# Cross-attention block with a mixture of experts: the dense expert stage is replaced by a two-phase dispatch of each token to its two experts

## The reference

```python
x = x + attention(layernorm(x), ctx, ctx, mask, Wq, Wk, Wv, Wo)
h = layernorm(x)
probs = softmax(h @ wg.T)                      # 8 experts
topk_w, topk_idx = top_k(probs, 2)
topk_w = topk_w / sum(topk_w)
expert_w = sum(one_hot(topk_idx, 8) * topk_w)  # zero for the six experts not chosen
y = sum over e of expert_w[e] * ((silu(h @ w1[e].T) * (h @ w3[e].T)) @ w2[e].T)
out = x + y
```

## Time and profile before

| | us |
|---|---|
| median of 3 runs (lowest, highest) | 327.93 (326.25, 330.78) |
| the profiled execution, own time | 327.75 |
| its span, first to last instruction | 325.9 |
| TensorE busy | 280.9 (86%) |
| VectorE busy | 262.5 (81%) |
| ScalarE busy | 176.2 (54%) |
| GpSimd busy | 125.1 (38%) |
| mean granted clock of TensorE, share of full speed | 0.966 |

### The profile page before, as it was taken

One profiled execution on the slowest core, in us unless ns is written; L12 is line 12 of the kernel. 1 busy time (PEld: TensorE's weight loads), 2 busy tenths in 40 slices (PEclk: granted clock), 3 DMA queues, 4 the chain that ended last, 5 costly groups with the idle time before them and its releaser, 6 DMA issues. The chain is left out here.

```text
span 325.9 us, 5240 instructions
## 1 busy us (share of the span) xinstructions
PE 280.9 (86%) x1689; PEld 209.9 (64%) x1689; DVE 262.5 (81%) x523; ACT 176.2 (54%) x312; POOL 125.1 (38%) x111
## 2 busy tenths in 40 slices
PE   1947788989898989798899889897898978999994
PEld 0823565667566757575668667785686856888882
DVE  6586965887588757797649999879998799999893
ACT  6891256546655665375664355552455534666551
POOL 5201250125011501131166556554565535666660
PEclk9995599999999999999997999999999999999998
DMA  5984503340333043430800003400134001240101
GB/s 151 283 232 100 126 2 82 91 120 3 93 87 81 2 96 84 111 119 18 257 4 1 0 1 108 155 0 0 34 112 149 0 2 32 88 173 2 32 0 32
DMA packets 32618, 24.96 MB, mean 77 GB/s; under 512 B 2984, under 2 KB 27184, under 8 KB 32592
## 3 DMA queue, kind: packets, MB, share of 16 engines
q1 hardware_dynamic: 31440, 23.08, 25.1%
q0 software_dynamic: 320, 1.05, 1.3%
q10 hardware_dynamic: 832, 0.51, 0.6%
HBM read 15.12 MB, written 1.11 MB: 50 GB/s over the span
## 5 line engine op out<-in xcount | busy, mean ns | idle before, releaser
L897 POOL TENSOR_TENSOR big<-big,raw 128x512 f32<-128x512 f32 x64 | 87.9, 1375 | 70.3 <-ACT big L819 59.0
L431 PE MATMUL bank<-st,bd 128*128 128x512 f32 x320 | 88.9, 402 | 11.8 <-DVE big L1205 11.7
L431 PEld LDWEIGHTS bank<-st,bd 128*128 128x128 f32 x320 | 58.3, 190 | 28.5 <-DVE big L1205 17.5
L660 ACT ACTIVATE st<-big 128x512 fp32r<-128x512 f32 x64 | 40.5, 632 | 50.3 <-DVE big L1205 49.7
L1180 DVE TENSOR_REDUCE m_neg<-bank 128x4 f32<-128x512 f32 x64 | 43.2, 682 | 20.3 <-PE bank L601 20.0
L1205 DVE TENSOR_TENSOR big<-big,bank 128x512 f32<-128x512 f32 x64 | 43.5, 679 | 12.0 <-POOL big L897 11.7
L632 PE MATMUL bank<-st,bd 128*128 128x512 f32 x150 | 51.8, 397 | 0.2 <-DVE m_bd L1193 0.2
L819 ACT ACTIVATE big<-bank 128x512 f32<-128x512 f32 x64 | 38.0, 593 | 24.7 <-PE bank L431 24.3
L1193 DVE TENSOR_TENSOR m_bd<-big,st 128x512 fp32r<-128x512 f32 x42 | 47.4, 1129 | 0.1
L790 ACT ACTIVATE big<-bank 128x512 f32<-128x512 f32 x64 | 37.5, 600 | 17.4 <-PE bank L587 17.1
L601 PE MATMUL bank<-bd,st 128*128 128x512 f32 x64 | 30.1, 496 | 7.0 <-DMA bd<-st 6.6
(11 more groups left out here) (119 smaller groups left out, 422.5 us busy)
## 6 DMA issues: line engine op xcount, KB each, us to landing
bd<-st SPq DMA_DIRECT2D x128, 64.0 KB, 2.1
raw<-ew_rows SPq DMA_DIRECT2D x32, 256.0 KB, 5.0
x_all<-in_x SPq DMA_DIRECT2D x4, 256.0 KB, 3.9
mask_i<-in_mask_BxS_if POOLq DMA_DIRECT2D x4, 256.0 KB, 4.5
ctx_all<-in_L_ffn_w SPq DMA_DIRECT2D x1, 1024.0 KB, 5.8
out<-ck SPq DMA_DIRECT2D x4, 256.0 KB, 2.3
ctx_all<-in_ctx SPq DMA_DIRECT2D x3, 256.0 KB, 4.4
ctx_all<-in_ctx ACTq DMA_DIRECT2D x1, 256.0 KB, 5.5
```

What stands on the lines that cost most here:

```text
L431: last = nc.tensor.matmul(o, w, m, start=(k == 0), stop=(k == len(pairs) - 1))
L660: return nc.scalar.activation(o, i, ACT.Copy)
L897: nc.gpsimd.tensor_tensor(silw[n % 3], sil[n % 3], ewb[:, k // 2, :], ALU.mult).then_inc(silw_ready, 1)
```

## The change

The attention rounds stay, and the expert stage is new. Each token is worked on only for its two experts. Its normalised row is scattered into a DRAM table at a place in its expert's region, together with the number of its (token, choice) pair in a 129th column; the table is then worked off in tiles of 128 rows, each of one expert; the results are scattered to DRAM by pair number, and at the end are gathered, weighted and added.

- There are two phases: the first takes quarters 0 to 2, the second quarter 3. As the number of tokens of an expert is not known when the program is built, each phase has as many tiles as could be needed in the worst case: (2\*1536 - 8)//128 + 8 = 31 and (2\*512 - 8)//128 + 8 = 15. All 46 are computed, whatever the counts. A tile past the end reads a block of filler rows.
- Routing on VectorE gets more steps: running sums of the selections over sequences (cum), which of the two choices each is (before, which), the row in the table (place_rows, with the counts of lower tokens from two products "rk" on TensorE), the weight of each choice (weigh), and per phase a table of the tiles, three parts (table). Routing of quarter 0 moves from the last round into the end of the round before it, that of quarters 1 and 2 from the expert stage into the last round, and that of quarter 3 lies beside the tiles 5 to 12. The normalised rows are written twice (two choices).
- In VectorE's last round the ticks now carry: place_rows(0) and the normalising of quarter 1 (tick 0), statistics of quarter 2 (1), weigh(0) (3), routing_step of quarter 1 (4 and 5), normalising of quarter 2 (7), place_rows(1) (8), weigh(1) (9), routing_step of quarter 2 (11 and 12), place_rows(2) and table part 0 (14), weigh(2) and part 1 (15), part 2 (16). Before they carried routing_step(0), the weights of quarter 0, and statistics and normalising of quarter 1 and statistics of quarter 2.
- GpSimd no longer multiplies. It issues 8 indirect DMAs a quarter (send) and one a tile (out to ys). The ones of quarter 3 are interleaved with tiles 5 to 12.
- SyncE opens a phase: 8 register values are loaded from `pad`, 9 DMAs of 128 rows of filler are issued, 31 (or 15) row numbers are loaded into registers, and the sends and the filler are waited for. Then it loads tiles, in a ring of XR = 8; tile n waits until the output of tile n - 8 has landed. The second phase is opened between tiles 23 and 24.
- TensorE, per tile: one transpose of the rows (turn_tile); for h1 and h3 together two products with 512 columns and two with 256 (hidden), where the tokens are now the stationary operand and the expert's matrix moves, its column from a register; two transposes of the gated result (turn_hidden); and six products with 128 columns of w2 moved, three for each half of the hidden channels (down), three tiles later.
- ScalarE, per tile: rounded copy of 128 columns, Silu of 256, rounded copy of 256, and a copy of the 128 columns that down has summed (take_rows).
- VectorE, per tile: two subtractions (128 and 256 columns) and the product of 256 columns.
- At the end SyncE gathers 8 pieces of 256 KB, VectorE does 32 operations of 128 columns, and four pieces are stored.

```diff
-LAG = 5
-RH = 6
+CT = 128
+PHASES = (3, NQ - 3)
+CAPS = [n * T for n in PHASES]
+NTS = [(2 * c - E) // CT + E for c in CAPS]
+NT = sum(NTS)
+XR, GR, YR = 8, 3, 6
...
 @block.sync
-            def spread_weights(q):
...
+            def open_phase(f):
+                sp.wait_ge(pad_ready, f + 1)
+                sp.dma_start(xg[f][E * REGS[f]:E * REGS[f] + CT, :], consts[:, C_PAD:C_PAD + RW]).then_inc(padded[f], 16)
+                _, at = nc.values_load_multi_w_load_instructions(pad[0:1, f, :], [mybir.EngineType.SP], ...)
+                for row in at:
+                    sp.dma_start(xg[f][bass.ds(row, CT), :], consts[:, C_PAD:C_PAD + RW]).then_inc(padded[f], 16)
+                sp.wait_ge(tab_ready, f + 1)
+                _, at = nc.values_load_multi_w_load_instructions(tab[0:1, 0, 32 * f:32 * f + NTS[f]], [mybir.EngineType.SP], ...)
+                for q in (range(3) if f == 0 else range(3, NQ)):
+                    sp.wait_ge(sent[q], 16 * 2 * QB)
+                sp.wait_ge(padded[f], 16 * (E + 1))
+                return list(at)
+            rows = open_phase(0)
+            for n in range(NT):
+                f = int(n >= NTS[0])
+                if n == NTS[0] - XR + 1:
+                    rows += open_phase(1)
+                if n >= XR:
+                    sp.wait_ge(t_full, n - XR + 1)
+                    sp.wait_ge(ysb_out[(n - XR) % YR], 16 * ((n - XR) // YR + 1))
+                sp.dma_start(xt[n % XR], xg[f][bass.ds(rows[n], CT), :]).then_inc(in_t[n % XR], 16)
...
 @block.tensor
+            def hidden(n):
+                pe.wait_ge(tlo_ready, n + 1)
+                if n >= 2:
                     pe.wait_ge(gg_ready, n - 1)
+                nc.tensor.matmul(both, t_lo[n % 2], first_high[:, :, bass.ds(col[n], I)], start=True, stop=False)
+                nc.tensor.matmul(both, t_hi[n % 2], first_high[:, :, bass.ds(col[n], I)], start=False, stop=False)
+                for k in range(2):
+                    last = nc.tensor.matmul(h[:, k * I:(k + 1) * I], t_hi[n % 2], first_low[k][:, bass.ds(col[n], I)],
+                                            start=False, stop=(k == 1))
+            def down(n):
+                pe.wait_ge(glo_ready, n + 1)
+                if n >= 1:
+                    pe.wait_ge(ysb_ready, n)
+                for c in range(2):
+                    piece = slice(c * P, (c + 1) * P)
+                    high, low = (second[:, k, bass.ds(col[n] + c * P, D)] for k in range(2))
+                    nc.tensor.matmul(yb[:, 0:D], g_hi[n % GR][:, piece], high, start=(c == 0), stop=False)
+                    nc.tensor.matmul(yb[:, 0:D], g_hi[n % GR][:, piece], low, start=False, stop=False)
+                    last = nc.tensor.matmul(yb[:, 0:D], g_lo[n % GR][:, piece], high, start=False, stop=(c == 1))
+            col = columns(0)
+            turn_tile(0)
+            for n in range(NT + 3):
+                if n + 1 < NT:
+                    turn_tile(n + 1)
+                if n == NTS[0]:
+                    col += columns(1)
+                if n < NT:
+                    hidden(n)
+                if n >= 3:
+                    down(n - 3)
+                if 1 <= n < NT + 1:
+                    turn_hidden(n - 1)
...
 @block.scalar
+            for n in range(NT + 3):
+                if n + 1 < NT:
+                    round_tile(n + 1)
...
+                    nc.scalar.activation(sil[n % 2], hb[n % 2][:, 0:I], ACT.Silu).then_inc(sil_ready, 1)
                 if n >= 3:
+                    take_rows(n - 3)
+                if 1 <= n < NT + 1:
                     round_hidden(n - 1)
...
 @block.gpsimd
+            for n in range(NT):
+                pool.wait_ge(ysb_ready, n + 1)
+                pool.wait_ge(in_t[n % XR], 16 * (n // XR + 1))
+                pool.indirect_dma_start(ys, bass.IndirectOffsetOnAxis(xt[n % XR][:, D:RW].bitcast(I32), 0), y_sb[n % YR], None, ...)
+                if 5 <= n < 5 + 2 * QB:
+                    send(QB * (NQ - 1) + (n - 5) // 2, (n - 5) % 2)
...
 @block.vector
+                            if tick == 0:
+                                place_rows(0)
+                                normalise(QB, NQ + 1)
...
+                            if tick == 14:
+                                place_rows(2)
+                                table(0, 0)
+                            if tick == 15:
+                                weigh(2)
+                                table(0, 1)
+                            if tick == 16:
+                                table(0, 2)
...
+            for b in range(B):
+                if b % QB == 0:
+                    dve.wait_ge(in_g[b // QB], 32)
+                own(nc.vector.scalar_tensor_tensor(acc[b % 2], got[:, 0, b, :], wgt[:, b, 0:1], x_all[:, b, :], ALU.mult, ALU.add))
+                ins = nc.vector.scalar_tensor_tensor(o_sb[:, b, :], got[:, 1, b, :], wgt[:, b, 1:2], acc[b % 2], ALU.mult, ALU.add)
```

More of the change, by code:

```diff
@@ L55 @@
 EPS = 1e-5
-LAG = 5
-RH = 6
 SH = 3
+CT = 128
[3 more added lines that the diff above has]
+NT = sum(NTS)
+NC = CAPS[0] // CT
+REGS = [c + CT for c in CAPS]
+RW = D + 1
+PAIRS = 2 * B * S
+IN_RANGE = "counts are at most the capacity of a region, and the table ends in a minimum with the last row or expert"
+XR, GR, YR = 8, 3, 6
 def split_constant(v):
@@ L183, in program @@
         wo_s = sb("wo_s", [P, D])
-        wg_hi = sb("wg_hi", [P, E], F32R)
-        wg_lo = sb("wg_lo", [P, E], F32R)
+        wgT = sb("wgT", [P, E])
+        cum = sb("cum", [P, B + 2, E])
+        before = sb("before", [P, QB, E])
+        which = sb("which", [P, QB, 2, E])
+        place = sb("place", [P, QB, E])
+        spread = sb("spread", [P, QB, 2, E])
+        rows_i = sb("rows_i", [P, B, 2], I32)
+        wgt = sb("wgt", [P, B, 2])
+        cnt = sb("cnt", [P, E])
+        tiles = sb("tiles", [P, E])
+        until = sb("until", [P, E])
+        tab = sb("tab", [P, 2, 48], I32)
+        pad = sb("pad", [P, 2, E], I32)
         bias_w = sb("bias_w", [P, P], F32R)
@@ new lines, in _ @@
+            rest_of_tile(0)
+            for n in range(NT + 1):
+                if n + 1 < NT:
+                    rest_of_tile(n + 1)
+                if n < NT:
+                    dve.wait_ge(sil_ready, n + 1)
+                    if n >= 2:
+                        dve.wait_ge(gT_full, n - 1)
+                    nc.vector.tensor_tensor(gg[n % 2], sil[n % 2], hb[n % 2][:, I:2 * I], ALU.mult).then_inc(gg_ready, 1)
+                if 1 <= n < NT + 1:
+                    rest_of_hidden(n - 1)
+                if n == 0:
+                    second_statistics(NQ - 1)
+                if n == 1:
+                    normalise(QB * (NQ - 1), 2 * NQ - 1)
+                if n == 5:
+                    routing_step(NQ - 1, 0)
+                    routing_step(NQ - 1, 1)
+                if n == 6:
+                    routing_step(NQ - 1, 2)
+                    routing_step(NQ - 1, 3)
+                if n == 8:
+                    place_rows(NQ - 1)
+                if n == 10:
+                    table(1, 0)
+                if n == 11:
+                    table(1, 1)
+                if n == 12:
+                    table(1, 2)
```

540 lines of the change are left out of this document (304 added, 236 removed).

## The result

The changed kernel takes 339.18 us (median of 4, 339.03 to 340.63) beside 328.31 for the kernel before (median of 4), a ratio of 1.034 with a 95% interval of 1.026 to 1.042. The forecast of 338 is met within its own range, but that the sum is met is luck: two of its terms are wrong by more than 10 us each and cancel. Measured again later, beside the last experiments, the changed kernel took 339.71 against 327.91, ratio 1.038 (1.035 to 1.041). One line of the profile's part 1 and four of its 40 slices of the changed kernel answer to the earlier trace rows. The profiled execution spans 339.0 us.

What follows compares the result with a forecast made beforehand. TensorE and VectorE were taken as bounds, counted stage by stage: first product at 187.7, tiles 114.1, extras 4, 6 and 3, end 21, sum 335.8, plus 1.85 outside the span: 338 us; own range 328 to 348, eight in ten 310 to 360.

Steps and rivals of the forecast that it cites:

- round 3, to `mT`: Attention round before the last: 7.3 us of VectorE work go in, about 2 us free, so +5 us.
- last round: Final attention round: VectorE's 37.5 us of work in a round of 27.2 us make it 13.3 us longer, bounds +7 to +20.
- With 3 us of its idle time left over: 40.5: Final attention round: VectorE has 37.5 us of work and keeps only 3 us idle, so the round takes 40.5 us.
- over 90% busy: Sign to look for in the final attention round: VectorE busy more than 90% of the time.
- the routing is hidden: Rival, attention rounds 3 and 4: VectorE's added work fits idle time, growth only 2 and 7 us, total 327; chance 0.15.
- I take that 0.22, as the row nearest in shape: Expert tiles on TensorE: each of six 128-column down products costs 0.22 us, 1.33 us a tile of 2.48.
- cheap products: Rival, expert tiles: down products cost 0.11 us, TensorE 1.82 a tile, ring decides at about 2.05, total 318; chance 0.25.
- The chain of 6.3 us: Tile loading: copy, GpSimd issue, write, SyncE issue and load take 6.3 us over 3.1 tiles, 2.03 a tile, just under TensorE.
- second opening: Before tile 24: SyncE issues nine fillers, waits and loads 23 registers; +6 us, with a TensorE hole of 5 us or more.
- The rival of 0.2 us a value: Rival, SyncE and TensorE at both phase openings: each register load takes 0.2 us, +6 us, total 344; chance 0.10.
- The end: After the last tiles: copy, output landing, gathers, 32 VectorE operations at 0.3 us and the last store take 21 us.
- the first tile at 188: Sign at the start of the expert stage: the first tile's product starts at about 188 us (187.7 in the sum).

Runs made afterwards that it cites:

- without the low product: The two products per tile of the rounded gated values with the low part of w2 left out of the changed kernel; 337.25 us, ratio 1.026.
- the kernel with both edits: Changed kernel with 15 ring places, second-phase fillers between loads of tiles 17 to 25, opening's waits at tile 31; 338.91 us on the second chip, 318.57 on the third.
- The run that was to separate the clock from the pieces: 49 unused 512-column products added to the changed kernel on TensorE, ahead of waits in the last round and before the first tile; 361.04 us, ratio 1.105.

## Why the prediction was right, and where it was wrong

The forecast's sum against the same places of the trace after:

| | forecast | measured | off by |
|---|---|---|---|
| round 3, to `mT` | +5 | +9.0 | +4 |
| last round | +13.3 | +24.8 | +11.5 |
| seam | +6 | +4.8 | -1 |
| first expert product | 187.7 | 201.94 | +14.2 |
| first to last `hidden`, 45 steps | 121.6 | 110.5 | -11.1 |
| last `hidden` to the end | 26.5 | 26.6 | 0 |
| span | 335.8 | 339.0 | +3.2 |

The forecast column of the tiles is 45 x 2.48 + 4 + 6; the last is 2.5 + 3 + 21. `mT` is what ends round 3; the timelines of VectorE before and after show it:

```profile
136.69 0.29 DVE L1093 COPY mT<-bank 128x128 f32<-128x128 f32 x1
```
```profile
145.64 0.29 DVE L1262 COPY mT<-bank 128x128 f32<-128x128 f32 x1
...
196.82 0.29 DVE L1121 TENSOR_TENSOR x_all<-bank,x_all 128x128 f32<-128x128 f32 x1 [1.64 <-PE bank L517]
```

**The last round: the step that failed first.** "With 3 us of its idle time left over: 40.5" held that VectorE would fill to the brim, "over 90% busy". Its work was counted nearly right; its idle time was not. Busy time by engine from `mT` to the end of attention, the kernel before and the changed kernel (columns as in the earlier trace rows):

```profile
136.69:163.40 26.71, 23.64 (x246) 17.23 (x245) 19.55 (x66) 17.50 (x38) 6.57 (x8) 1.00 0.44 131
```
```profile
145.64:197.11 51.47, 36.82 (x269) 28.16 (x267) 35.18 (x134) 21.02 (x43) 30.45 (x32) 0.73 0.19 49
```

VectorE is busy for 35.2 us, where the forecast had 37.5, but in a stretch of 51.5 us: 68%. Its idle time was 7.2 us and grew to 16.3, where the forecast let it shrink to 3. What the runs showed in its place: the routing lies in unbroken pieces, TensorE waits behind them for the division of a head, and VectorE then waits for TensorE's chain in turn. Timeline of TensorE, one of these waits in round 3 and two in the last round:

```profile
140.88 0.48 PE L512 MATMUL bank<-cst,on 128*128 128x128 f32 x1 [5.94 <-DVE on L1130]
...
183.09 0.47 PE L512 MATMUL bank<-cst,on 128*128 128x128 f32 x1 [3.26 <-DVE on L1130]
...
193.15 0.33 PE L512 MATMUL bank<-cst,on 128*128 128x128 f32 x1 [2.46 <-DVE on L1130]
```

Round 3 went over its +5 in the same way. VectorE's busy time from 108.5 us to `mT` rose by 7.0 us (21.1 to 28.1), close to the 7.3 that were counted, but its idle time grew from 7.1 to 9.0 us instead of giving 2 away. Routing of quarter 0 stands there from 133.18 to 140.18 us, and TensorE's wait of 5.94 us is behind it.

In the one execution that was profiled, 4.2 us of work more made the last round 4.5 to 5.0 longer, which shows VectorE's work to be on the path; the later routing steps point the same way, weakly. The forecast's rival "the routing is hidden" is wrong.

A second thing was missed, the clock. In 142.8 to 185.0 the granted clock averages 0.70, where the earlier trace rows have 1.00. It falls to 0.50 (1.2 GHz) during the wait of 5.94 us and lies there from 138 to 156 us, and again at 183 to 188, beside the 3.26 us at 183.09. What it costs can be read in part from seven profiled executions that have the same attention code: the changed kernel twice, the ring of 15 twice, the kernels without the low product and with early fillers, and the kernel with both edits in the third set. In the three with a mean clock of 0.73 in the last round it takes 50.9 to 51.5 us, in the other four, 0.78 to 0.81, 49.0 to 50.4. So 0.08 of the clock goes with about 2.3 us. Carried on in a straight line to 1.00 that would be some 8 of the 11.5 us, an estimate from these seven; none of them shows the round at the full clock, and a round with shorter waits may have the higher clock for that reason. The run that was to separate the clock from the pieces couldn't.

**The tile on TensorE: the second, other way.** "I take that 0.22, as the row nearest in shape" is refuted: 0.11, the pace of the 8-column row. A product of 128 float32r columns costs no more than one of 8. Each product has a weight load, and the weight loads start 0.11 us apart beside both (138.33 and 138.44 us before, 233.24 and 233.35 after); that they set the pace is read from this, not tested. At a granted clock of 0.50 the products start 0.21 us apart (211.50 to 211.71). The rival "cheap products" had this right; its price, 20 us, wasn't paid out, as its own text said in part ("the ring decides with about 2.05"). A tile is 1.69 on TensorE (forecast of that rival 1.82) and 2.46 in the mean.

**The ring.** The chain of 6.3 us came out: copy 0.28, GpSimd 0.97, landing of an output 2.4, of a load 2.0 (medians). With TensorE at 1.69 the ring therefore decides, as the rival "cheap products" had it at 2.05: after the second opening, where no sends are in the way, the 19 turns from 272.08 to 310.81 us are 2.04 apart, 1.96 without the one at 283.30, behind which TensorE loads its registers for the second phase. What no bound had is what stands in the same queues beside it: the sends on GpSimd, which delay each output, the second opening, and VectorE's work on quarter 3 at the start (forecast +4, 7.6 over the pace in tiles 0 to 5). Given 15 buffers instead of 8, SyncE's wait falls by more than half, and together with the fillers and the later waits of the opening 21 us come back. So the tiles' mean of 2.46 came out as forecast (2.48, and 2.70 with the lumps) by luck, for another reason: the ring, GpSimd and VectorE's pieces, not TensorE. The run without the low product supports it, with 10 us of TensorE gone and 2 us of time.

**GpSimd.** 1.0 us for an indirect DMA was close for its busy time (0.97), but 0.30 of issue follows. Eight sends at the seam start 1.28 apart, and while quarter 3 is sent, beside tiles 5 to 12, a tile has a send and an output, 2.55 us where TensorE needs 1.69. Timeline of GpSimd:

```profile
232.33 0.97 POOL L1016 DMA_INDIRECT ys<-big  x1 [0.30 <-issue]
233.60 0.97 POOL L1002 DMA_INDIRECT xg<-rows,rows_i  x1 [0.30 <-issue]
234.88 0.97 POOL L1016 DMA_INDIRECT ys<-big  x1 [0.30 <-issue]
```

That pace was not among the bounds of the tile (GpSimd "about 1"), and with a ring of 8 the tiles keep to it until the eight sends are out (outputs from 232.33 to 250.20 us, 2.55 apart). The Trainium skill (DMA: Bandwidth & Descriptors, Latency and other measured facts) gives about 1 us to the first byte for a DMA that GpSimd describes in software; no run here shows the first byte. The busy time of 0.97 us is near that figure, but the pace is set by the 1.28 us from one start to the next.

**The second opening.** Forecast +6 with a hole of 5 us or more; the gap between outputs is 10.25, 8.6 above the pace, and the run with early fillers gave 5 back. Right in place and mechanism.

**The register loads.** The rival of 0.2 us a value is wrong. Between the end of the filler at L438 (256.29) and the first of L442 (257.09) SyncE loads 8 values, 0.80 us, 0.10 each; at the first opening the same eight take 1.26 us (186.25 to 187.51), 0.16 each. The Trainium skill (Runtime: NRT & Kernel Launch, Instruction fetch mechanics) has 200 ns a register; the measurement, below that at both places, decides.

**The end.** 26.6 against 26.5. Of it the gathers and the 32 operations are as counted: the first operation of VectorE stands 6.16 us for `raw`, and from then on each pair takes 0.65 us, for 16 pairs 10.4 (9.6 forecast). Timeline of VectorE:

```profile
325.64 0.35 DVE L1426 SCALAR_TENSOR_TENSOR big<-raw,wgt,x_all 128x128 f32<-128x128 f32 x1 [6.16 <-DMA raw<-ys]
326.30 0.35 DVE L1426 SCALAR_TENSOR_TENSOR big<-raw,wgt,x_all 128x128 f32<-128x128 f32 x1
```

The forecast called itself wrong if the first tile's product came before 178 or the tiles every 2 us or less; neither happened in the changed kernel. The signs of "over 90%" and "the first tile at 188" were wrong, and they said what the total didn't.

## What to carry to other kernels

Replacing a stage that one engine fills by one with two fifths less of its work (busy 89.5 us instead of 146.3) gained nothing here until the queue that feeds it ran ahead: count for each tile what every queue issues, DMA issues of GpSimd among them, and look at how the ring's depth places the other waits on the same queue. Two waits in series on one queue can hide each other: each edit alone returned 7 and 5 us, and both, with the opening's waits moved too, 21. The sum of a stage's idle time doesn't say what work it can take in; here 15.6 us more of VectorE's work made the last round 24.8 longer. Whether shorter pieces would fit better was tried only with two routing steps, and that run's 3 us aren't explained.

## What the runs showed of the hardware that was not expected

- Products of 128 float32r columns start 0.11 us apart, as those of 8 columns do.
- The granted clock fell to 0.50 during a wait of 5.94 us of TensorE and lay there for some 18 us (138 to 156). The same last round took 51.2 us in the mean of three executions with a mean clock of 0.73 and 49.0 in the two with 0.81.
- An indirect DMA of 128 rows holds GpSimd for 0.97 us, and the next can start only 1.28 us after the last.
- One program ran at 338.9 us on one chip and at 318.6 on another, with the kernel before at 328.0 and 327.9 there. On the slower one ScalarE stood 7.1 to 9.2 us with a remote releaser, until 201.6 to 205.7 us, in all four kernels of that set. While it stands, rows are being sent and fillers written; whether that has a part in it isn't known, and chip and time of measuring weren't separated. A kernel's variants have to be held against each other on one chip, and a surprising one repeated on a second.
